# A quarter's tokens in three tiles of 128 lanes instead of four of 96, and a residual buffer that is loaded with bias and text

## The chip, the cores and the metric

The kernel runs on one NeuronCore of a Trainium2 chip. The metric is device time in microseconds for one execution; each kernel is run several times, and the median counts. The profiled execution is one more run, with the hardware profiler on. PE is TensorE (matmuls) and PEld its weight loads, DVE is VectorE, ACT is ScalarE, POOL is GpSimd, SP is SyncE, which here issues DMAs.

## The reference

Sixteen images of 3 x 128 x 128 and a text of 32 tokens for each go through one block of width 192. Cut to what matters:

```python
t = conv16x16(x) + conv_b                       # (16, 64, 192): 64 patches an image
h = attention(t, heads=12, head_dim=16)         # q, k, v, softmax, values
h = h @ wo.T + bo                               # (16, 64, 192)
h = concatenate([h, txt], axis=1)               # (16, 96, 192)
h = h + mamba(layernorm(h))                     # in-projection to 2 x 384, causal conv of 4 taps, silu,
                                                # selective scan with 16 states along the 96 tokens, gate, out-projection
h = h + ffn(layernorm(h))                       # below
# ffn: two "bitlinear" layers with ternary weights and activations rounded to 8 bits per token
x_q = round_to_8_bits(rmsnorm(h, g_in));  up, gate = split(x_q @ w_in_q.T)      # 2 x 512
y   = silu(gate) * up
out = round_to_8_bits(rmsnorm(y, g_out)) @ w_out_q.T
```

Each image has L = 96 tokens in h: 64 of the image (NP) and 32 of the text (NT). The layer norms, the rounding scales and the feed-forward work on one token at a time; only attention and the mamba mixer (convolution and scan) mix tokens, and only within an image.

## The kernel before

**Tiles.** The work after attention is cut into NQ = 4 quarters of QB = 4 images, so QT = 384 tokens. The mixer holds its data with channels on the lanes and the 384 tokens of a quarter along the columns, in CT = 3 tiles of 128 channels. The residual h, the layer norms and the feed-forward hold tokens on the lanes: one tile for each image, 96 lanes, four tiles a quarter. `h` is [96, 16, 192]: lanes 0 to 63 are written by `add_bo` (attention's projection plus the bias `bo_bc`), lanes 64 to 95 by one DMA of the text.

**The front.** SP issues all loads in one queue, in the order written. TensorE computes the patch embedding for two halves of the images, then one small matmul `wsum` (it sums the absolute feed-forward weights over lanes, and waits for VectorE's reduce of those weights, lines 1180 and 1181), then q, k and v. Attention runs over PAIRS = 8 pairs of images in a loop that is staggered over the engines: `scores(i)`, `values(i-2)`, `turn_prob(i-1)`, `project(i-3)`, `turn_out(i-2)` on TensorE, `softmax_in`, `softmax_out` and `add_bo` on VectorE, `block_keys` on GpSimd. `project(p)` multiplies the turned attention output of each of the two images (64 columns each) with wo. The first quarter's normalization and projections are woven in from i = 5, and the second quarter's normalization follows attention (its steps are negative).

**The steps.** The selective scan of one quarter takes 24 steps (3 channel tiles times 8 pairs of states), 96 in all. A step g is: `times_b` on GpSimd (line 455), `decay` on ScalarE (two exponentials, line 994), `scan` on VectorE (line 1291), `guards` on ScalarE (two tanh, line 1003) and `guard_states` on VectorE (1297, 1300), the product with C on GpSimd (461) or for three of eight steps on VectorE (1306), and `sum_y` on TensorE (808). All other work is placed beside the steps by hand: the tables MIXER and FFN give for each piece the step at which its engine does it, counted from the start (MIXER) or from the end (FFN) of its quarter's scan. So the feed-forward of quarter q runs beside the scan of quarter q+1, and that of the last quarter after all steps. SCALAR_WORK counts ScalarE's extra instructions of a step. If their sum is 4 or more, the guards of later steps are not computed ahead there:

```python
upto = min(STEPS, g + (1 if scalar_work(g) >= 4 else 3), guarded + 2)
while guarded < upto:
    guards(guarded)
    guarded += 1
beside(g)
```

A planner (`banks_of_jobs`) gives every TensorE job of these tables the PSUM bank that comes free first by the tables' due steps; a job waits for the last reader of the job before it in its bank. Three banks serve the jobs during the steps.

**The feed-forward of a quarter**, in order: `out_proj` (TensorE, two jobs) and `add_out` (VectorE, line 1317), `spread` (bn_stats and bn_aggr, 1323 and 1326), `root_in` (GpSimd, 467), `center` and `gain_in` (GpSimd, 477 and 483; for the last quarter `center_last` on VectorE, 1335), `max_in` (1377), `scale_in` (GpSimd, 490 to 495), `quant_in` (ScalarE, 1012), `turn_q1` (transposes, 769) and `q1_out` (1022), the gate and up matmuls (583, two each of 512 columns), `silu_gate` (1032), `times_up` (1384), `square` (1039), `gain_out` (GpSimd, 499; last quarter VectorE, 1357), `max_out` (1388), `mean_square` and `scale_out` (GpSimd, 506 to 524; last quarter partly VectorE, 1363 to 1367), `quant_out` (1045), `turn_q2` (787), `q2_out` (1052), `ffn_out` (583) and `finish` (1396), then `store` (SP, 374). Nearly all of these are one instruction for each tile of tokens, so four a quarter. The layer norm in front of the mixer is `spread_b` (1239, 1242), `root` (430 to 433), `normed` (933), `turn` (709), `turned` (940).

## Time and profile before

| | |
|---|---|
| Median of 3 runs | 544.12 us (543.4 to 544.31) |
| Profiled execution | 544.86 us, of it the span from first to last instruction 543.0 us |
| PE busy | 409.1 us (75%) |
| VectorE busy | 415.1 us (76%) |
| ScalarE busy | 349.2 us (64%) |
| GpSimd busy | 373.5 us (69%) |
| Mean granted TensorE clock | 0.874 |

A share of busy time is an average over the front, the steps and the tail. In all rows times are microseconds from the start of the span, durations microseconds or, where marked, nanoseconds. "idle before" is the time that the engine stood still just before the instruction, and the arrow names what ended it. A granted clock of 1.00 is TensorE at 2.4 GHz, 0.50 is 1.2 GHz.

### The profile page before, as it was taken

The page shows a single profiled execution, that of the slowest core. Times are in us where ns is not written, and L with a number is a line of the kernel's source. Part 1 is how long each engine was busy: PE and PEld are TensorE (multiplying, and loading weights), DVE is VectorE, ACT ScalarE, POOL GpSimd, SP SyncE. Part 2 cuts the span into 40 slices and gives each one's busy share as a digit, 9 for nine tenths or more (in the row PEclk, how much of TensorE's full clock was granted, in tenths as well). Part 3 has the DMA queues.
Part 4 walks back from the last instruction along what each step waited for, and adds up shares of the span by engine and source line. Part 5 has one row for each costly group of instructions (what it writes and reads, how often), then busy time and mean ns, then how long its engine had stood idle before and what let it go on. Part 6 is the DMA issues. An engine that isn't in the chain of part 4 may idle for free.

```text
span 543.0 us, 5369 instructions
## 1 busy us (share of the span) xinstructions
PE 409.1 (75%) x1588; PEld 233.1 (43%) x1588; DVE 415.1 (76%) x513; ACT 349.2 (64%) x627; POOL 373.5 (69%) x290
## 2 busy tenths in 40 slices
PE   5999996877975959996577799867656854857664
PEld 1336664544532425563243456534323632423533
DVE  3242556234899999899999989799899899798543
ACT  1135444228678669678489869968966866992362
POOL 2025630017869889799879999987799999977410
PEclk9999999686989779997988899787878989986966
DMA  8900000047000037200003440000244000000000
GB/s 312 233 1 1 2 0 2 0 160 308 1 4 1 1 116 264 85 4 0 2 0 143 164 159 4 11 12 0 116 174 174 2 22 1 1 1 0 7 16 22
DMA packets 10414, 34.30 MB, mean 63 GB/s; under 512 B 2208, under 2 KB 5104, under 8 KB 10160
## 3 DMA queue, kind: packets, MB, share of 16 engines
q1 hardware_dynamic: 9984, 33.17, 17.5%
q10 hardware_dynamic: 400, 0.79, 0.4%
q8 instruction: 13, 0.21, 0.2%
q14 instruction: 17, 0.14, 0.1%
HBM read 32.57 MB, written 1.38 MB: 63 GB/s over the span
## 4 chain that ended last, share of the span: by engine, by line
POOL 30%; DVE 12%; issue 11%; ACT 11%; PE 9%; ACTq 0%; DVEq 0%; POOLq 0%
POOL big L455 14%; POOL big L461 9%; DVE PS L1291 5%; PE PS L583 4%; ACT PS L994 3%; ACT big L1003 3%; PE PS L808 3%; POOL big L499 2%; DVE big L1300 1%; PE PS L732 1%; DVE big L1306 1%; ACT L994 1%; ACT big L1045 1%; DVE big L1384 1%; PE PS L787 1%
## 5 line engine op out<-in xcount | busy, mean ns | idle before, releaser
L808 PE MATMUL PS<-big,eighth 128*128 128x384 f32 x384 | 172.1, 587 | 69.3 <-POOL big L461 68.7
L1291 DVE TENSOR_TENSOR_SCAN PS<-PS,big 128x768 f32<-128x768 f32 x96 | 168.5, 1755 | 17.2 <-ACT PS L994 14.8
L455 POOL TENSOR_TENSOR big<-big,bc 128x768 f32<-128x768 f32 x96 | 173.4, 1820 | 0.0
L808 PEld LDWEIGHTS PS<-big,eighth 128*128 128x128 f32 x384 | 83.2, 227 | 140.7 <-POOL big L461 88.5
L461 POOL TENSOR_TENSOR big<-big,bc 128x768 f32<-128x768 f32 x60 | 109.2, 1821 | 39.7 <-DVE big L1300 39.5
L994 ACT ACTIVATE PS<-big,Aneg 128x384 f32<-128x384 f32 x192 | 103.7, 572 | 41.7 <-DVE big L1306 28.4
L1003 ACT ACTIVATE big<-big,guard,Ahalf 128x380 f32<-128x380 f32 x192 | 122.2, 690 | 0.0
L1300 DVE SCALAR_TENSOR_TENSOR big<-big,PS 128x768 f32<-128x768 f32 x60 | 57.0, 950 | 5.8 <-ACT big L1003 0.5
L420 POOL TENSOR_TENSOR big<-bc,cst_sb 96x1536 f32<-96x1536 f32 x8 | 22.0, 2752 | 43.3 <-ACT bc L903 32.2
L583 PE MATMUL PS<-big,w_in_sb 96*128 96x384 f32 x96 | 43.8, 597 | 5.0 <-DVE big L1252 4.4
L583 PE MATMUL PS<-big 128*64 128x34 f32 (+3 forms) x416 | 43.7, 282 | 0.0
L583 PEld LDWEIGHTS PS<-big 96*64 96x64 f32 (+2 forms) x416 | 30.5, 145 | 16.3 <-issue 14.6
L1297 DVE SCALAR_TENSOR_TENSOR PS<-big,PS 128x768 f32<-128x768 f32 x36 | 34.6, 961 | 3.8 <-DVE PS L1291 0.5
L430 POOL TENSOR_SCALAR rstd<-bmv 96x4 f32<-96x4 f32 x4 | 1.8, 460 | 48.8 <-DVE bmv L1242 48.7
L1306 DVE TENSOR_TENSOR big<-PS,bc 128x768 f32<-128x768 f32 x36 | 34.1, 948 | 0.4
L583 PEld LDWEIGHTS PS<-big,w_in_sb 96*128 96x128 f32 x96 | 21.7, 232 | 21.8 <-issue 13.1
L805 PE MATMUL PS<-big,diagD 128*128 128x384 f32 x24 | 13.6, 658 | 22.4 <-DVE big L1312 22.4
L583 PE MATMUL PS<-bc 128*96 128x512 f32 x48 | 22.4, 630 | 6.4 <-DMA bc<-in_cw_dram 6.4
L732 PE MATMUL PS<-big,diagW 128*128 128x384 f32 (+3 forms) x72 | 24.3, 480 | 0.0
L1045 ACT ACTIVATE big<-big,magic 96x512 f32<-96x512 f32 x14 | 10.5, 804 | 21.1 <-POOL big L523 15.3
L1209 DVE TENSOR_REDUCE big<-PS 128x12 f32<-128x768 f32 x8 | 7.6, 952 | 21.5 <-PE PS L583 21.5
L1104 ACT ACTIVATE big<-PS 128x768 f32<-128x768 f32 x8 | 6.5, 808 | 26.8 <-PE PS L648 26.8
(151 smaller groups left out, 538.8 us busy)
## 6 DMA issues: line engine op xcount, KB each, us to landing
bc<-bc_rows SPq DMA_DIRECT2D x32, 768.0 KB, 4.3
bc<-in_x_cols_dram SPq DMA_DIRECT2D x3, 512.0 KB, 6.5
bc<-in_x_cols_dram SPq DMA_DIRECT2D x1, 1536.0 KB, 8.7
out_dram<-h SPq DMA_DIRECT2D x4, 288.0 KB, 2.7
big<-in_f_in_dram SPq DMA_DIRECT2D x1, 768.0 KB, 10.8
bc<-in_cw_dram ACTq DMA_DIRECT2D x1, 576.0 KB, 5.6
w_in_sb<-in_w_in_dram SPq DMA_DIRECT2D x1, 576.0 KB, 14.4
big<-in_f_out_dram SPq DMA_DIRECT2D x1, 384.0 KB, 11.9
```

The lines of the kernel that those rows point to most:

```text
L420: P.tensor_tensor(kbd[:, p % 2], kT[:, hf, :, c:c + 128].unsqueeze(2).broadcast_to([F, 2, HPT, 128]), headmask.unsqueeze(1).unsqueeze(3).b ...
L455: P.tensor_tensor(pair(vR[:, g % VRING]), part(du, q, m).unsqueeze(1).broadcast_to([128, PAIR, QT]), rows_of(g, 0), ALU.mult).then_inc(sem ...
L461: P.tensor_tensor(v, v, rows_of(g, 1), ALU.mult).then_inc(sem("c_pool"), 1)
L583: return pe.matmul(o_, l_, r_, start=start, stop=stop)
L732: ins = pe.matmul(o_[:, :, s:L], diagW[:, j, KW - 1 - s, :], xi[:, :, 0:L - s], start=False, stop=s == KW - 1, skip_group_check=True)
L808: ins = pe.matmul(y_sum, eighth[:, :], vR[:, g % VRING, QT * e:QT * (e + 1)], start=False, stop=True, skip_group_check=True)
L994: ins = A.activation(state_of(g, e), part(delta, q, m), ACT.Exp, scale=Aneg[:, PAIR * j + e, m:m + 1])
L1003: ins = A.activation(gR[:, g % GRING, QT * e:QT * (e + 1)].rearrange("p (b l) -> p b l", b=QB)[:, :, 0:L - 1], lt[:, :, 1:L], ACT.Tanh, bi ...
L1291: V.tensor_tensor_scan(h_, h_, vR[:, g % VRING], 0.0, ALU.mult, ALU.add).then_inc(sem("scan_done"), 1)
L1297: V.scalar_tensor_tensor(states(g), gR[:, g % GRING], 1.0, states(g), ALU.add, ALU.mult).then_inc(sem("guarded_here"), 1)
L1300: V.scalar_tensor_tensor(vR[:, g % VRING], gR[:, g % GRING], 1.0, states(g), ALU.add, ALU.mult).then_inc(sem("guarded"), 1)
L1306: V.tensor_tensor(pair(vR[:, g % VRING]), pair(states(g)), rows_of(g, 1), ALU.mult).then_inc(sem("c_vector"), 1)
```

## The change

The 384 tokens of a quarter are laid out without a gap: token t of the quarter is lane t mod 128 of tile t div 128, so there are NTL = 3 tiles of 128 lanes, and an image may lie in two of them. Everything that holds tokens on the lanes follows: h is [128, 12, 192], and xn, xq, sg, yf, the statistics and the scales have three tiles. The transposes are 128 wide, and the jobs of out_proj, q1, q2 and the down projection hold two tiles in the first and one in the second. In the tables the gates are all at step 14 (the fourth was at 15), and SCALAR_WORK has 3 for 4 where a piece lost an instruction (5 for 6 for silu).

The bias is no longer added from a buffer. h is loaded with bias rows (five DMAs) and text rows (four DMAs), all in front of the loads of the feed-forward weights. `project` multiplies whole tiles of 128 tokens: aoT holds the four images of a quarter with 96 columns each, the text's columns set to zero once by GpSimd, so that the product is zero there. Even pairs do tile 0, odd pairs tiles 1 and 2, and `add_bo` adds the product to what h holds.

```diff
+NTL = QT // 128
-for b in range(QB):
-    FFN.update({"gate%d" % b: 14 + b // 3, "up%d" % b: 16 + b // 2, "times%d" % b: 17 + b // 2, "square%d" % b: 18 + b // 2,
-                "gain%d" % b: 19 + b // 2, "max%d" % b: 21 + b // 2})
+for i in range(NTL):
+    FFN.update({"gate%d" % i: 14, "up%d" % i: 16 + i // 2, "times%d" % i: 17 + i // 2, "square%d" % i: 18 + i // 2,
+                "gain%d" % i: 19 + i // 2, "max%d" % i: 21 + i // 2})
-SCALAR_WORK = dict(xn=4, turned=2, ..., quant_in=4, q1_out=2, silu=6, square0=1, square1=1,
-                   square2=1, square3=1, quant_out0=2, quant_out1=2, q2_out0=2, q2_out1=2)
+SCALAR_WORK = dict(xn=3, turned=2, ..., quant_in=3, q1_out=2, silu=5, square0=1, square1=1, square2=1, quant_out0=2,
+                   quant_out1=1, q2_out0=2, q2_out1=1)
...
-        g_in_bc = sb("g_in_bc", [F, D])
-        g_out_bc = sb("g_out_bc", [F, FH])
-        bo_bc = sb("bo_bc", [NP, D])
+        g_in_bc = sb("g_in_bc", [128, D])
+        g_out_bc = sb("g_out_bc", [128, FH])
...
-        h = sb("h", [L, NB, D])
+        h = sb("h", [128, NQ * NTL, D])
...
-        aoT = carve(256, F).rearrange("p (m t) -> p m t", m=2)
+        aoT = carve(2 * QT, F).rearrange("p (m b l) -> p m b l", m=2, b=QB)
...
+        def tiles(q, i=slice(0, NTL)):
+            return h[:, NTL * q:NTL * (q + 1)][:, i]
...
             load("wo", wo_sb, wo)
-            load("wo", bo_bc[:, :], bo.partition_broadcast(NP))
+            parts = h[:, :, :].rearrange("p (q i) d -> p q i d", i=NTL)
+            text = txt.rearrange("(q b) l d -> b l q d", b=QB)
+            for i, rows, n in ((0, 0, 64), (0, 96, 32), (1, 0, 32), (1, 64, 64), (2, 32, 64)):
+                load("txt", parts[rows:rows + n, :, i, :], bo.unsqueeze(0).unsqueeze(0).broadcast_to([n, NQ, D]))
+            for b, i, rows in ((0, 0, 64), (1, 1, 32), (2, 2, 0), (3, 2, 96)):
+                load("txt", parts[rows:rows + NT, :, i, :], text[b])
             load("ffn", f_in_raw, f_in.rearrange("p m n -> p (m n)"))
             load("ffn", f_out_raw, f_out.rearrange("p m n -> p (m n)"))
-            load("txt", h[NP:L, :, :], txt.rearrange("b l d -> l b d"))
...
             link(P.memset(vbd, 0.0))
+            link(P.memset(aoT, 0.0))
...
             def project(p):
-                for b2 in range(2):
+                turned_all = aoT.rearrange("p m b l -> p m (b l)")
+                for k, i in enumerate((1, 2) if p % 2 else (0,)):
                     for m in range(2):
-                        ins = mm(project_out[:, D * b2:D * b2 + D], aoT[:, m, 64 * b2:64 * b2 + 64], wo_sb[:, m, :],
+                        ins = mm(project_out[:, D * k:D * (k + 1)], turned_all[:, m, 128 * i:128 * (i + 1)], wo_sb[:, m, :],
                                  m == 0, m == 1)
...
             def out_proj(q, j):
-                for b2 in range(2):
-                    t = L * (2 * j + b2)
+                for k, i in enumerate((2,) if j else (0, 1)):
                     for m in range(CT):
-                        ins = mm(o_[0:L, D * b2:D * b2 + D], part(sres, q, m)[:, t:t + L], w_out_sb[:, m, :],
+                        ins = mm(o_[:, D * k:D * (k + 1)], part(sres, q, m)[:, 128 * i:128 * (i + 1)], w_out_sb[:, m, :],
                                  m == 0, m == CT - 1)
...
             def normed(q):
-                for b in range(QB):
-                    ins = A.activation(xn[:, b, :], h[:, QB * q + b, :], ACT.Identity, bias=nmr[:, b:b + 1],
-                                       scale=rstd[:, b:b + 1])
+                for i in range(NTL):
+                    ins = A.activation(xn[:, i, :], tiles(q, i), ACT.Identity, bias=nmr[:, i:i + 1], scale=rstd[:, i:i + 1])
...
             def add_bo(p):
                 dve.wait_ge(sem("wo_ps"), p + 1)
-                V.tensor_tensor(h[0:NP, 2 * p:2 * p + 2, :], project_out.rearrange("p (b c) -> p b c", b=2),
-                                bo_bc[:, :].unsqueeze(1).broadcast_to([NP, 2, D]), ALU.add).then_inc(sem("h_sb"), 1)
+                if p == 0:
+                    dve.wait_ge(sem("ld_txt"), 16 * LOADS["txt"])
+                here = tiles(p // 2, slice(1, 3) if p % 2 else slice(0, 1))
+                n = 2 if p % 2 else 1
+                V.tensor_tensor(here, project_out[:, 0:D * n].rearrange("p (i c) -> p i c", i=n), here, ALU.add
+                                ).then_inc(sem("h_sb"), 1)
```

All other functions of the feed-forward and of the normalization change in the same way as out_proj and normed: loops over three tiles of 128 lanes for loops over four of 96, in the same order and with the same waits.

## Rows read from the trace of the kernel before

**Rows 1.** Busy time of each engine in one stretch of steps; then clock, DMA share, GB/s.

```profile
232.00:329.00 97.00, 75.41 (x228) 42.63 (x227) 92.73 (x98) 75.49 (x139) 88.15 (x73) 0.89 0.18 66
```

The columns are: stretch, its length, busy us (and instructions) of PE, PEld, DVE, ACT and POOL, granted clock, DMA share, GB/s.

**Rows 2.** Groups of instructions by line, steps only (129 to 504 us).

```profile
L461 POOL TENSOR_TENSOR big<-big,bc 128x768 f32<-128x768 f32 x60 | 109.2, 1821 | 39.7 <-DVE big L1300 39.5
```

**Rows 3.** The chain that ended last, in the steps: start, us, what.

```profile
246.01 1.47 POOL big L477
...
253.60 1.76 POOL big L483
...
285.09 1.14 DVE bst L1239 x4
...
458.12 1.86 ACT big L1012 x4
...
460.96 2.42 ACT big L1003 x4
...
468.79 2.41 ACT big L1032 x4
...
491.36 2.45 POOL big L499 x2
```

**Rows 4.** DMA queues and DMA issues with size and us to landing.

```profile
q1 hardware_dynamic: 9984, 33.17, 17.5%
...
h<-in_txt_dram SPq DMA_DIRECT2D x1, 384.0 KB, 13.4
```

**Rows 5.** The timeline of the loads: start, us, engine, line, what.

```profile
9.29 0.47 SPq L346 DMA_DIRECT2D h<-in_txt_dram  x1
...
20.65 2.28 DVE L1180 TENSOR_REDUCE wsum<-big 96x1 f32<-96x2048 f32 x1 [6.93 <-DMA big<-in_f_out_dram]
...
22.85 0.94 DVE L1181 TENSOR_REDUCE wsum<-big 128x1 f32<-128x768 f32 x1
...
28.72 0.28 PE L583 MATMUL PS<-wsum,ones 128*128 128x2 f32 x2
```

**Rows 6.** The timeline of TensorE and ScalarE in attention, and one output projection.

```profile
66.06 1.51 PE L583 MATMUL PS<-big 96*64 96x192 f32 x8
...
94.90 2.78 PE L583 MATMUL PS<-big,w_in_sb 96*128 96x384 f32 x4 [3.36 <-DVE big L1252]
...
102.64 1.48 PE L648 MATMUL PS<-cst_sb,big 128*128 128x128 f32 x6
...
122.73 1.86 ACT L933 ACTIVATE big<-h,nmr,rstd 96x192 f32<-96x192 f32 x4 [3.11 <-POOL nmr L433]
...
332.61 2.11 PE L583 MATMUL PS<-w_out_sb,big 128*96 128x192 f32 x12
```

**Rows 7.** Busy time and granted clock in three short stretches, columns as in rows 1.

```profile
94.90:106.00 11.10, 11.10 (x46) 7.13 (x46) 0.91 (x3) 1.86 (x2) 0.00 (x0) 0.54 0.00 0
...
302.50:324.90 22.40, 22.37 (x65) 13.09 (x66) 20.25 (x21) 14.89 (x30) 21.99 (x18) 0.92 0.49 177
...
517.30:525.80 8.50, 8.22 (x24) 4.27 (x24) 2.03 (x4) 6.39 (x11) 0.00 (x0) 0.54 0.01 2
```

**Rows 8.** The timeline of the tail.

```profile
507.05 2.93 ACT L1045 ACTIVATE big<-big,magic 96x512 f32<-96x512 f32 x4 [13.83 <-POOL big L523]
...
512.53 1.39 DVE L1335 SCALAR_TENSOR_TENSOR big<-h,big,g_in_bc 96x192 f32<-96x192 f32 x4
...
518.90 6.70 PE L583 MATMUL PS<-f_in_q,big 96*96 96x512 bf16 x16
...
528.76 2.45 DVE L1388 TENSOR_REDUCE big<-big 96x1 f32<-96x512 f32 x4
...
530.05 0.20 POOL L510 TENSOR_TENSOR big<-big 96x4 f32<-96x4 f32 x1
...
532.91 2.88 PE L787 MATMUL PS<-cst_sb,big 96*128 96x96 f32 x16 [7.31 <-ACT big L1045]
...
535.59 2.76 PE L583 MATMUL PS<-f_out_q,big 128*96 128x192 bf16 x16
```

More of the change, by code:

```diff
@@ L551, in beside @@
                         scale_in(q)
-                for b in range(QB):
+                for b in range(NTL):
                     for q in due("gain%d" % b, g):
@@ L707, in turn @@
                     o_ = begin("turn", q, m)
-                    for b in range(QB):
-                        ins = pe.transpose(o_[0:F, L * b:L * b + L], xn[:, b, F * m:F * (m + 1)], ident[0:L, 0:L])
+                    for i in range(NTL):
+                        ins = pe.transpose(o_[0:F, 128 * i:128 * (i + 1)], xn[:, i, F * m:F * (m + 1)], ident)
                     done(ins, "turn")
@@ L834, in beside @@
                 for kind in ("gate", "up"):
-                    for b in range(QB):
+                    for b in range(NTL):
                         for q in due("%s%d" % (kind, b), g):
@@ L1010, in quant_in @@
                 act.wait_ge(sem("q1_scale"), q + 1)
-                for b in range(2 if q == LAST else QB):
-                    ins = A.activation(xq[:, b, :], xq[:, b, :], ACT.Identity, bias=magic[0:L, 0:1],
+                for b in range(2 if q == LAST else NTL):
+                    ins = A.activation(xq[:, b, :], xq[:, b, :], ACT.Identity, bias=magic[:, 0:1],
                                        scale=st[:, q, 6, b:b + 1])
-                    if b % 2:
+                    if b:
                         ins.then_inc(sem("q1_ready"), 1)
@@ L1078, in beside @@
                 for q in due("silu", g):
-                    for b in range(QB):
+                    for b in range(NTL):
                         silu_gate(q, b)
-                for b in range(QB):
+                for b in range(NTL):
                     for q in due("square%d" % b, g):
@@ L1087, in beside @@
                             quant_out(q, 2 * half)
-                            quant_out(q, 2 * half + 1)
+                            if half == 0:
+                                quant_out(q, 1)
                 for half in range(2):
@@ L1091, in beside @@
                         q2_out(q, 2 * half)
-                        q2_out(q, 2 * half + 1)
+                        if half == 0:
+                            q2_out(q, 1)
             for i in range(PAIRS + 3):
@@ L1237, in spread_b @@
                     dve.wait_ge(sem("xn_ready"), q)
-                for b in range(QB):
-                    ins = V.bn_stats(bst[:, b, :], h[:, QB * q + b, :])
+                for b in range(NTL):
+                    ins = V.bn_stats(bst[:, b, :], tiles(q, b))
                 link(ins)
-                for b in range(QB):
+                for b in range(NTL):
                     ins = V.bn_aggr(bmv[:, b, :], bst[:, b, :])
@@ L1314, in add_out @@
             def add_out(q, j):
[L1315 removed]
                 job_here(dve, "out", q, j)
[L1317 to L1318 removed]
+                here = tiles(q, slice(2, 3) if j else slice(0, 2))
+                n = 1 if j else 2
+                V.tensor_tensor(here, job_bank("out", q, j)[:, 0:D * n].rearrange("p (i c) -> p i c", i=n), here, ALU.add
+                                ).then_inc(sem("left_out"), 1)
             def spread(q):
                 job_left(dve, "out", q, 1)
[L1322 to L1323 removed]
+                for b in range(NTL):
+                    ins = V.bn_stats(dst[:, b, :], tiles(q, b))
                 link(ins)
[L1325 removed]
+                for b in range(NTL):
                     ins = V.bn_aggr(dmv[:, q, b, :], dst[:, b, :])
@@ L1435, in after @@
                         quant_in_last(q)
-                for b in range(QB):
+                for b in range(NTL):
                     for q in due("times%d" % b, g):
                         times_up(q, b)
-                for b in range(QB):
+                for b in range(NTL):
                     for q in due("gain%d" % b, g):
@@ L1442, in after @@
                             gain_last(q, b)
-                for b in range(QB):
+                for b in range(NTL):
                     for q in due("max%d" % b, g):
```

164 lines of the change are left out of this document (77 added, 87 removed), and 6 rows, old and new, of the table PE_JOBS.

## The prediction, written before the kernel was changed

> **What bounds the kernel now.** I read the windows by stage first, then the groups of instructions inside the step stage, then the chain that ended last, and the timeline only where the chain runs through work that the change touches. The kernel has three stages. The front (patch embedding, attention, the first quarter's projections) lasts until the first scan at 129 us. The steps (96 of them, 24 a quarter) last until 504.3, and the tail (feed-forward of the last quarters) until 543.0.
>
> In the steps VectorE is nearly full: 92.7 of 97.0 us in the stretch of the second quarter, with GpSimd at 88.2 and ScalarE at 75.5 [rows 1]. In the 375 us of steps GpSimd's product with C waits 40 us for VectorE [rows 2]. So VectorE sets the pace most of the time, GpSimd is close behind, and each small feed-forward instruction between two steps delays a scan or a product. The chain shows the same: it changes engine, and it passes through feed-forward work wherever that stands in front of a step's own work [rows 3]. In the tail there are no steps left to hide anything. The chain runs through single instructions in turn, with TensorE near half its clock, 0.54 and so mostly at the lower of its two levels [rows 7, 8].
>
> **The front: loads.** Before, one load of the bias (48 KB) and, behind the feed-forward weights, one of the text (384 KB, 512 packets of 768 bytes). After, nine loads ahead of those weights: 1,024 packets of bias and 512 of text. The weights are what DVE sums at 20.65, when the last of them lands; the sum ends at 23.79 and TensorE needs it at 28.72 for its small matmul, ahead of all of q and k [rows 5]. That is 4.9 us; TensorE loads the weights of that matmul 0.4 earlier, so the slack is 4.5 us. The text was issued at 9.29 [rows 5] and landed after 13.4 [rows 4], at 22.7. It lies directly behind the weights that landed at 20.65, so its 512 packets took 2.1 us, 4.1 ns each. By that the weights land later by 512 + (1,024 − 64) = 1,472 packets, 6.0 us: **TensorE waits 1.5 us**. Lower bound: under 3.1 ns a packet there is no wait at all, 0. Upper bound: the mean packet of the queue in the whole execution, over 3 KB, took 0.175 × 543 × 16 / 9,984 = 152 ns of one engine of 16, or 9.5 ns [rows 4]. A packet of 768 bytes should not cost more: 14.0 us, a wait of 9.5 us. I take the row of the text, which is the same kind of packet. The seven more issues on SP (about 0.5 us each, as the text's 0.47 [rows 5]) are passed while the queue has older data to move. What stands behind the wait: all q and k, then all of attention, so the wait counts in full.
> The text load priced a packet at 4.1 ns [rows 4, 5]. The Trainium skill (DMA: Bandwidth & Descriptors, section "Why small descriptors are slow") gives a fixed overhead of about 3 cycles beside 32 bytes a cycle, which makes 27 cycles of 850 MHz for 768 bytes, an estimate of 2.0 ns over 16 engines. By that the weights would be 2.9 us late, inside the slack, and the forecast 1.5 us lower.
>
> **The front: attention.** In its steady part TensorE runs without a gap, and a projection of a pair is four matmuls (eight records) in 1.51 us, the records 0.18 apart [rows 6]. After, even pairs have two matmuls and odd ones four. They load 128 columns of weights where they loaded 64. The mixer's output projection, with 96 columns of weights and the same 192 moving, had twelve records in 2.11, again 0.18 each [rows 6], so I price the wide ones at 0.18 too. Four even pairs save 0.72 each: −2.9. The project of pair 6 lies ahead of pair 7's transpose in TensorE's order, so it counts too. Bound: if wider loads showed, +0.05 a record, it would be −0.5 less for the even pairs and 1.6 more for the odd ones, −0.8 in all. Behind attention lies the normalization of the second quarter, which the first scan waits for: four bn_stats become three (−0.28) with one bn_aggr less (−0.1), by the group of four in 1.14 [rows 3], and xn 4 to 3 of 1.86 [rows 6], −0.5. The six wide transposes cost what eight narrow ones did (low clock: 1.48 for six of 128 columns [rows 6]). Normalization −0.9, and together with the loads the front gives −2.9 − 0.9 + 1.5 = **−2.3**. Hidden at nothing: the memset of aoT, one instruction of 768 columns on GpSimd, which then idles until the keys are there (uncovered it would be under 2 us, by g_out's 512 columns in 1.22 [rows 3]), and the wider g loads.
>
> **The steps.** I take the pieces on the chain [rows 3] one by one. I price an instruction of GpSimd, VectorE or ScalarE by its columns, not by its lanes, so a group of four becomes three, and a width of 768 becomes 576. Bound: if 128 lanes cost more than 96 in proportion, nothing is saved here (rival B). For columns speaks GpSimd's product on 96 lanes and 768 columns, 1.76, beside the product with C on 128 lanes and 768, 109.2 / 60 = 1.82 [rows 2, 3].
> - center 1.47 and gain_in 1.76, once each in the shown quarter and again in the third (440.3, 445.3): −0.36 and −0.44, twice: −1.6
> - bn_stats four in 1.14: −0.28
> - quant_in, four in 1.86: −0.46
> - silu, four in 2.41: −0.60
> - second pair of gain_out, two in 2.45 at 491.4: −1.22
> - The weights in SCALAR_WORK: quant_in goes from 4 to 3 and so under the threshold of 4. ScalarE then does a guard ahead of quant_in, in a wait for GpSimd's scales, and not two behind it. At 460.96 four guard activations in 2.42 become two: −1.2.
>
> Sum **−5.4**. Bounds: off the chain too the work shrinks, by about 7.7 us on VectorE (12 to 9 each of the products with up and the maxima, the statistics, add_out, max_in, finish) and 6.1 on GpSimd, so no more than −7.7. At the other end the neighbours just off the chain hold the pace, and one guard now precedes xn at step 18: 0 to +0.8. I take the chain's own sum: it is the sum of what stood in front of a step. The gates of a quarter all come at step 14 and the bank planner has one job less to seat, so I see no new wait for a bank.
>
> **The tail**, from the scales at 507.05 [rows 8]. quant_out 4 to 3 of 2.93: −0.73; two q2_out of 512 columns for 384: +0.2. center 4 to 3 of 1.39, one finish less, the maximum over 576: −0.33 − 0.33 − 0.2. First q1 transposes (four, now 128 wide, 0.25 for 0.19 at low clock) and their eviction: +0.34. So TensorE begins the gates 1.05 earlier. Its 16 records of 512 columns in 6.70, 0.427 each, become 12: −1.71. Then three gains and maxima for four on VectorE, −1.23, but GpSimd's mean square ends at 530.25 where VectorE's maxima end at 531.22. Only 0.97 counts, then GpSimd ends last. q2 transposes 16 in 2.88, now 12 of 128 columns at 0.247: +0.08. Down projection 16 records of 0.16 to 12: −0.64. Last finish one for two: −0.33. Sum: **−4.6**. Bounds: −5.5 if GpSimd's first small operations, slow beside VectorE's gains, speed up; −3 if the wider transposes and evictions show twice.
>
> **Sum.** −2.3 − 5.4 − 4.6 = −12.3 us against a span of 543.0 with 1.9 us around it (544.86). The median shown is 544.12, 0.74 lower; I put the same difference on it: **531.8 us**, 2.3% faster. What a measurement tells from no change is 0.2%, 1.1 us.
>
> **The rivals.**
> - *A, the loads hurt.* The bias packets cost up to the mean packet, and TensorE waits 4 to 9.5 us: 534 to 539.8. For it: the loads are in front, the queue is full until 26 us, all 1,024 packets read the same 768 bytes. Against it: the text's rate. 0.13.
> - *B, the steps give nothing.* The engines are coupled, and what one saves it waits for the other, as it does for 40 us already [rows 2]: 531.8 + 5.4 = 537.2. For it: VectorE and GpSimd are only 5 us apart in 97 [rows 1]. Against it: both lose work. 0.15.
> - *C, more than the chain shows.* VectorE's whole 7.7, no wait in front: 528; and if attention keeps TensorE's clock up at 94.9 to 106, where it ran 11.1 us at 0.54 [rows 7], up to 4 less: 525. 0.12.
> - *D, slower: TensorE's clock.* Place: the steps with the convolutions of the next quarter. From 302.5 to 324.9 TensorE was busy 22.37 of 22.40 at 0.92 [rows 7], so it is the bound there. In the front TensorE was idle for 3.4 us before 94.9 [rows 6], and at 0.54 for the next 11 us though never idle [rows 7]. The change takes TensorE work out just before these steps. If one such stretch ran at half clock, it would take 22.4 × 0.92 / 0.5 = 41.2, +18.8: 550.6. From 12.3 us of it the kernel is slower. Against it: the four-matmul groups right after the idle there recover in one step. 0.08. The Trainium skill (TensorE: Matmul & The Clock Gate, section "HAM oscillation") states that gaps between bursts of matmuls throw the clock back to half; the front's rows agree.
>
> The forecast itself has 0.52, with its own range 529 to 535 (the load 0 to 3, the steps −7.7 to −3). The range that is to hold 8 in 10 reaches over A, B and C: 525 to 540. Faster: the forecast, A, B, C, less 0.01 for A and B together, 0.91; same 0.02; slower, most of D, 0.07.
>
> **What would show it.** In the trace after: the reduce of f_in begins near 26.7 (not 20.65) and the matmul with wsum near 30.3. The projections of even pairs have four records. First scan near 127. Per quarter nine matmuls of out_proj, three gates, three ups. The last scan's quarter ends near 497, gates in the tail 12 records, tail from the last gate to the end 34 us for 38.7. Wrong would be: a wait above 4 us at wsum; GpSimd's or VectorE's idle time in the steps up by 5 us; a granted clock below 0.8 in the steps' windows.

## The result

The changed kernel took 541.70 us (median of 20 runs, 536.07 to 545.06), the kernel before 545.08 beside it (20 runs, 543.03 to 550.84). The ratio is 0.9901, 95% interval 0.9876 to 0.9926: 1.0% faster, where 2.3% were forecast, and the median lies 1.7 us above the range. (Ratios, and below the median of e15_all_back, leave out the few executions that ran disturbed, so a ratio is not the quotient of the two medians.) The profiled execution took 541.64 with a span of 539.8; before it was 544.86 and 543.0.

**The loads.** First the timeline of the changed kernel: start, us, engine, line, what.

```profile
7.28 3.29 SPq L350 DMA_DIRECT2D h<-in_bo_dram  x5
10.61 5.89 SPq L350 DMA_DIRECT2D h<-in_txt_dram  x4
16.54 3.72 SPq L350 DMA_DIRECT2D big<-in_f_in_dram  x1
20.31 3.71 SPq L350 DMA_DIRECT2D big<-in_f_out_dram  x1
...
37.31 2.28 DVE L1192 TENSOR_REDUCE wsum<-big 96x1 f32<-96x2048 f32 x1 [23.62 <-DMA big<-in_f_out_dram]
39.51 0.94 DVE L1193 TENSOR_REDUCE wsum<-big 128x1 f32<-128x768 f32 x1
...
40.50 0.59 PE L593 MATMUL PS<-wsum,ones 128*128 128x2 f32 x2 [10.70 <-DVE wsum L1193]
```

The feed-forward weights land at 37.31 where they landed at 20.65 [rows 5], and TensorE stands still for 10.70 us. Then the windows of the same kernel: stretch, length, VectorE busy (and instructions), granted clock, DMA share, GB/s.

```profile
12.00:14.00 2.00, 1.69 (x9) 1.00 1.04 304
14.00:16.00 2.00, 0.00 (x0) 1.00 0.52 135
16.00:18.00 2.00, 0.00 (x0) 1.00 0.20 46
18.00:20.00 2.00, 0.00 (x0) 1.00 0.17 60
20.00:22.00 2.00, 0.00 (x0) 1.00 0.16 50
22.00:24.00 2.00, 0.00 (x0) 1.00 0.26 53
24.00:26.00 2.00, 0.00 (x0) 1.00 0.31 72
26.00:28.00 2.00, 0.00 (x0) 1.00 0.57 176
28.00:30.00 2.00, 0.00 (x0) 1.00 1.09 180
30.00:32.00 2.00, 0.00 (x0) 1.00 1.05 208
32.00:44.00 12.00, 6.48 (x12) 0.50 0.72 158
44.00:60.00 16.00, 3.17 (x5) 0.95 0.00 1
```

From 16 to 26 us, while the bias comes in, the queue moves about 56 GB/s with its engines busy for 0.22 of the time. Behind TensorE's idle time the granted clock is 0.50 until past 44, so the first projections run at the lower of its two levels.

**The tail** of the changed kernel, by the timeline, beside [rows 8]:

```profile
507.20 0.56 DVE L1326 TENSOR_TENSOR big<-PS,big 128x384 f32<-128x384 f32 x1 [3.53 <-PE PS L817]
...
509.66 2.23 ACT L1053 ACTIVATE big<-big,magic 128x512 f32<-128x512 f32 x3 [12.97 <-POOL big L533]
...
520.48 5.30 PE L593 MATMUL PS<-f_in_q,big 96*128 96x512 bf16 x12 [0.41 <-ACT big L1030]
...
531.81 2.82 PE L797 MATMUL PS<-cst_sb,big 128*128 128x128 f32 x12 [6.02 <-ACT big L1053]
...
534.56 2.10 PE L593 MATMUL PS<-f_out_q,big 128*128 128x192 bf16 x12
...
536.06 1.07 DVE L1410 SCALAR_TENSOR_TENSOR h<-PS,big,h 128x192 f32<-128x192 f32 x3 [4.62 <-PE PS L593]
```

Compare starts and sizes. The gates, 16 records in 6.70 us, are 12 in 5.30. They began 1.58 later than before; the down projection 1.03 earlier.

Three points cut the execution into stages: TensorE's matmul with wsum, the first scan, and VectorE's last gate by z (L1326, before L1312).

| stage | before | after | change | forecast |
|---|---|---|---|---|
| start to wsum matmul | 28.72 | 40.50 | +11.8 | +1.5 |
| wsum matmul to first scan | 100.40 | 99.29 | −1.1 | −3.8 |
| first scan to last gate by z (the steps) | 375.20 | 367.41 | −7.8 | −5.4 |
| last gate by z to end (the tail) | 38.68 | 32.60 | −6.1 | −4.6 |
| span | 543.0 | 539.8 | −3.2 | −12.3 |

The steps and the tail gave more than forecast. The loads took most of it back, and the lower clock behind them hides what attention gave in the second row; both are taken apart below. Each column is one profiled execution. In GpSimd's row of [rows 2] little moved:

```profile
L471 POOL TENSOR_TENSOR big<-big,bc 128x768 f32<-128x768 f32 x60 | 109.5, 1824 | 37.3 <-DVE big L1314 37.1
```

It waits 37.3 us for VectorE, not 39.7: the steps are shorter, and in this row the same engine is waited for.

### The profile page after: what moved, and what is told of

The parts are those of the page before. It is cut to its first block, busy times and chain, and to the rows that moved or that the text cites. A ratio compares the mean times of both kernels' runs of the same rounds, so it can differ in the third digit from the quotient of the medians.

```text
span 539.8 us, 5082 instructions
## 1 busy us (share of the span) xinstructions
PE 397.8 (74%) x1484; PEld 222.7 (41%) x1484; DVE 399.8 (74%) x481; ACT 338.3 (63%) x601; POOL 367.3 (68%) x288
## 4 chain that ended last, share of the span: by engine, by line
POOL 31%; DVE 11%; PE 9%; issue 9%; ACT 6%; DVEq 0%; ACTq 0%; POOLq 0%
POOL big L465 15%; POOL big L471 10%; DVE PS L1305 5%; PE PS L817 4%; PE PS L593 3%; POOL big L509 2%; ACT PS L1001 2%; DVE big L1314 1%; PE PS L743 1%; DVE big L1320 1%; POOL big L447 1%; DVE big L1399 1%; ACT big L1053 1%; ACT big L1010 1%; PE PS L797 1%
## 5 line engine op out<-in xcount | busy, mean ns | idle before, releaser
L817 PEld LDWEIGHTS PS<-big,eighth 128*128 128x128 f32 x384 | 81.9, 224 | 144.8 <-POOL big L471 93.6
L471 POOL TENSOR_TENSOR big<-big,bc 128x768 f32<-128x768 f32 x60 | 109.5, 1824 | 37.3 <-DVE big L1314 37.1
L593 PEld LDWEIGHTS PS<-big 128*64 128x64 f32 (+3 forms) x400 | 31.6, 155 | 15.6 <-issue 15.3
L440 POOL TENSOR_SCALAR rstd<-bmv 128x3 f32<-128x3 f32 x4 | 1.9, 464 | 46.5 <-DVE bmv L1256 46.4
L1053 ACT ACTIVATE big<-big,magic 128x512 f32<-128x512 f32 x11 | 8.4, 805 | 18.8 <-POOL big L533 14.2
## 6 DMA issues: line engine op xcount, KB each, us to landing
h<-in_bo_dram SPq DMA_DIRECT2D x3, 192.0 KB, 15.1
```

The costliest lines, as they stand in the source:

```text
L471: P.tensor_tensor(v, v, rows_of(g, 1), ALU.mult).then_inc(sem("c_pool"), 1)
L593: return pe.matmul(o_, l_, r_, start=start, stop=stop)
L817: ins = pe.matmul(y_sum, eighth[:, :], vR[:, g % VRING, QT * e:QT * (e + 1)], start=False, stop=True, skip_group_check=True)
```

## Experiments on the front: which packets, and why

Four kernels, each the changed one with only the nine loads altered.

*e1_last*: the nine loads behind all others.

```
-            parts = ...; for i, rows, n in ...: load("txt", ...)   (nine loads)
             load("ffn", f_in_raw, ...)
...
             load("g", g_out_bc[:, :], g_out.partition_broadcast(128))
+            parts = ...; for i, rows, n in ...: load("txt", ...)   (the same nine)
```

> The changed kernel with its nine bias and text loads moved behind all other loads; nothing else. Theory (the nine loads in front of the FFN weights cost the whole front loss, and the rest of the change is worth what the first scan to the end showed, 13.9 us): FFN weights land near 20.6, the wsum matmul is near 28.7, the q/k projections run at the clock of the kernel before, the first scan is at 125 to 127, and the span is 527 to 530 (about 529 to 532 as a time), 2.3 to 2.9% under the kernel before. Rival (the front loss comes from the attention or from the clock on its own): the first scan stays near 139.8 and the time near 541. Rival (a late start gave the steps their gain, so it is lost with the stall): first scan near 126, but steps and tail give back only 10, span near 533.

*e2_distinct*: the same destinations, other sources.

```
-    load("txt", parts[rows:rows + n, :, i, :], bo.unsqueeze(0).unsqueeze(0).broadcast_to([n, NQ, D]))
+    load("txt", parts[rows:rows + n, :, i, :], txt.rearrange("b l d -> (b l) d")[0:NQ * n].rearrange("(q n) d -> n q d", q=NQ))
```

> The changed kernel, its five bias loads in place with the same destinations and the same 1,024 packets of 768 bytes, but each packet reads a row of its own (rows of the text tensor) instead of the one bias row: the true bias is left out. Theory (many packets that read the same 768 bytes are slow): the FFN weights land at 21 to 27, the first scan is 8 to 13 us earlier than in the changed kernel (127 to 132), time 529 to 534. Rival (packet count, or the small lane ranges of the nine loads): no change, FFN weights near 37, time near 541.

*e3_one*: one bias load in place of five, `load("txt", h[:, 0:8, :], bo...broadcast_to([128, 8, D]))`, text into `h[32 * b:32 * (b + 1), 8:12, :]`.

> The changed kernel with the five bias loads joined into one over all 128 lanes and two thirds of h (the same 1,024 packets of the same row) and the four text loads put into the last third of h (the same 512 packets); bias and text lie at wrong places. Theory (same address): FFN weights land at 33 to 38 as in the changed kernel. Rival (number of loads, or narrow lane ranges): they land at 21 to 27 and the first scan comes 8 us or more earlier.

*e4_bias_last*: only the five bias loads behind the others.

> The changed kernel with the five bias loads behind all other loads, the four text loads still in front. Theory (same address): the text loads cost only their packets, 512 at 4 to 9.5 ns, 2 to 5 us: FFN weights at 21 to 26, first scan 125 to 129, time 528 to 533. Rival (lane ranges of 32, packet count): FFN weights at 25 to 30, a third to half of the loss stays.

What was measured; of the front, the start of the sum over f_in (weights landed), the wsum matmul and the first scan; e1_last timed in 6 runs (the profiled one, 525.86, is the fastest of them), the others once, which is why the landing of the weights and not the time decides here:

| kernel | weights | wsum matmul | first scan | span | time |
|---|---|---|---|---|---|
| before | 20.65 | 28.72 | 129.12 | 543.0 | 544.86 |
| changed | 37.31 | 40.50 | 139.79 | 539.8 | 541.64 |
| e1_last | 20.36 | 28.60 | 124.60 | 524.1 | 526.85 (525.86 to 531.50) |
| e2_distinct | 26.94 | 30.19 | 126.85 | 527.1 | 528.88 |
| e3_one | 36.92 | 40.11 | 141.07 | 541.5 | 543.35 |
| e4_bias_last | 21.37 | 29.42 | 126.06 | 525.7 | 527.55 |

The ratio of e1_last to the kernel before is 0.9661 (0.9614 to 0.9708), and its span is 3 us under the 527 to 530 expected. What lay behind the stall was not lost with it: from the first scan to the end it took 399.50, the changed kernel 400.01. The two readings that decide are these. The timeline and a window of e2_distinct, columns as above:

```profile
26.94 2.28 DVE L1192 TENSOR_REDUCE wsum<-big 96x1 f32<-96x2048 f32 x1 [12.85 <-DMA big<-in_f_out_dram]
```

```profile
14.00:26.00 12.00, 0.09 (x1) 1.00 1.09 237
```

And the windows of e3_one; its columns are stretch, length, busy us (and instructions) of PE, PEld, DVE, ACT and POOL, clock, DMA share, GB/s:

```profile
16.00:18.00 2.00, 2.00 (x6) 0.78 (x5) 0.00 (x0) 0.00 (x0) 0.00 (x0) 1.00 0.30 59
18.00:20.00 2.00, 2.00 (x6) 0.69 (x5) 0.00 (x0) 0.68 (x1) 0.00 (x0) 1.00 0.53 52
```

With 1,024 different source rows the queue is full and moves 237 GB/s. With the one row it moves 46 to 72, whether the packets go out in five narrow loads or in one over all 128 lanes. So neither the number of loads, nor their lane ranges, nor the count of packets is the cause, but their source: all 1,024 read the same 768 bytes of bo. Against e2_distinct the weights are 10.4 us later, 10.1 ns for each bias packet. In e4_bias_last, with only the text in front, the weights landed at 21.37; in the ten traces with no such load in front, at 20.1 to 20.8. The 512 text packets by themselves cost about 1 us, 2 ns each. Then two more.

*e6_rows4*: the bias loads' source becomes `txt[0, 0:NQ, :].unsqueeze(0).broadcast_to([n, NQ, D])`.

> The changed kernel, its bias loads in place with the same destinations and 1,024 packets of 768 bytes, but the four quarters of h read four different neighbouring rows (one block of 3,072 bytes, each row 256 times) instead of one row 1,024 times; the true bias is left out. With one row the loads ran at 50 to 60 GB/s and the weights landed at 37.3, with 1,024 different rows at 26.9. Theory (the reads queue at the one place in memory that holds the row, so four rows serve four times as fast): full rate or nearly, weights at 26.9 to 29, time 528 to 532. Rival (any source read again and again is slow): weights at 35 to 37, time 540 to 542.

*e9_before_loads*: the kernel before and one load.

```
+            load("txt", h[0:NP, :, :], bo.unsqueeze(0).unsqueeze(0).broadcast_to([NP, NB, D]))
             load("ffn", f_in_raw, ...)
```

> The kernel before plus one load in front of the feed-forward weights: the bias row into 64 lanes and 16 rows of h, 1,024 packets of 768 bytes that all read one row; it is overwritten later, so the result is the same. Theory (these packets alone are the front's loss, at 12 to 14 ns each): weights land 11 to 14 us later (32 to 35), less 4.5 of slack, so first scan 7 to 13 us later with the low clock behind the stall, span 550 to 556. Rival (the loss needs the change's other parts): under 2 us.

In e6_rows4 the weights landed at 25.82: four neighbouring rows, each read 256 times, are as quick as 1,024 different ones. It is enough that the reads are spread over 3,072 bytes instead of 768; why, no run here shows. One rival is left: e2_distinct and e6_rows4 read the text tensor, and no run reads one row of it 1,024 times, so the place where bo lies is not told apart from the repetition. The front of e6_rows4 was good (first scan 125.57), and yet it took 532.15 us; the steps were longer, and a section below says by what. In e9_before_loads one load of the same row made the kernel before 12.9 us longer (span 555.9, time 557.77): weights at 36.12, wsum matmul at 39.32, first scan at 141.96. So the load alone does it, 15.5 us for 1,024 packets or 15.1 ns each, and nothing else of the change is needed. That is more than was expected for the weights (32 to 35) and the upper end for first scan and span. How busy the engines show says little here. One of its windows, columns as in the first table of windows:

```profile
18.00:20.00 2.00, 0.00 (x0) 1.00 0.62 53
```

That is 53 GB/s at a share of 0.62, where the changed kernel moved 60 at 0.17.

**The clock behind the stall.** From the wsum matmul to the first scan e1_last, e2_distinct and e4_bias_last took 96.00, 96.66 and 96.64 us; the changed kernel and e3_one, where TensorE had stood idle for 10.7 and 10.9 us, took 99.29 and 100.96. In the kernel before it took 100.40, and 102.64 in e9_before_loads. So behind the stall it took 2.2 to 4.4 us more, 2.7 in the changed kernel, and there the granted clock stood at 0.50 before it came back to 1.00 by 46. The Trainium skill (TensorE: Matmul & The Clock Gate, section "HAM oscillation") states that idle gaps throw the clock to half; the trace agrees, 1.00 before the gap and 0.50 behind it.

## Experiments on the steps: whose work was it

*e7_nudge* tests a single place. Twelve times VectorE sums delta over the later positions with a scan on 384 columns (L1283, the suffix scan here; 0.92 us at its shortest). Before, one of them took 5.23 us, by the timeline:

```profile
256.25 5.23 DVE L1283 TENSOR_TENSOR_SCAN big<-keep,big 128x384 f32<-128x384 f32 x1
```

In the changed kernel the same one took 1.36, and the suffix scan behind it came 4.1 us earlier, counted from the first scan, where this one came 0.5 earlier. Edit, on e1_last, in gain_in:

```
+                if q == 0:
+                    P.tensor_tensor(spare[:, :], g_out_bc[:, 0:D], g_in_bc[:, :], ALU.mult)
                 P.tensor_tensor(xq, xq, g_in_bc[:, :].unsqueeze(1)..., ALU.mult)
```

> The changed kernel with its nine loads last, plus one GpSimd product of 192 columns (0.4 to 0.6 us, into a spare tile) just ahead of the gain of quarter 0, so that this stretch of GpSimd is about as long again as with 768 columns; the result is the same. Theory (3.6 us of the gain in the steps come from one place: before, VectorE's suffix scan at 256.25 was held for 5.2 us behind three GpSimd products in a row, and the shorter gain lets it in between them): the suffix scan near 251.6 takes about 5 us again, the scans after it are 3.5 to 4.5 us later, span 527.5 to 528.5 for 524.1. Rival (the gain comes from the work taken out and not from the meeting): the suffix scan stays at 1.3 us and the span grows by 0 to 0.6.

The nudge did not bring the hold back: the suffix scan took 1.89 us, and from the first scan to the end e7_nudge took 399.81 for 399.50. So it doesn't tell what a hold there costs. e9_before_loads does, as it is the kernel before in its steps. That scan took 1.75 in it (its longest were 4.24 and 2.84 elsewhere), and its steps took 375.99 for 375.20. Such a hold comes and goes with small shifts, and this one place isn't what the change saved. Holds as a whole may have a part in it, which no run isolates: the twelve suffix scans together took 21.2 us in the kernel before and 20.9 in e9_before_loads, and 17.6 to 19.6 in the kernels with the change, but for the two in which one took over 8 us.

That it is a hold is best seen in e6_rows4, by the timeline of VectorE and GpSimd:

```profile
169.46 2.64 POOL L447 TENSOR_TENSOR big<-big 128x1152 f32<-128x1152 f32 x1
170.07 8.13 DVE L1297 TENSOR_TENSOR_SCAN big<-keep,big 128x384 f32<-128x384 f32 x1
172.04 1.82 POOL L471 TENSOR_TENSOR big<-big,bc 128x768 f32<-128x768 f32 x1
173.81 3.58 POOL L465 TENSOR_TENSOR big<-big,bc 128x768 f32<-128x768 f32 x2
```

A scan that takes 0.92 alone started behind a GpSimd product and ended at 178.20, 0.8 after the fourth of four that followed each other without a gap. From the first scan to the last gate by z this kernel took 370.54, the others of its kind 366.8 to 367.8, 3 us too much. Its tail took 34.19 for 32.6, but that is no hold: its last output projection took 5.76 us for 3.17, at the lower clock (more on this below). The Trainium skill (SBUF — State Buffer, section "Who interferes with whom") states that a VectorE instruction with two SBUF inputs contends with a GpSimd instruction that reads SBUF, and calls what they share an exclusive lock. The trace agrees: keep and delta both lie in SBUF. That GpSimd then keeps the turn through four instructions no page says, and no run here isolates it.

*e8_guard* tests the prediction's −1.2 for the order of the guards. Edit, on e1_last: `xn=3` to `xn=4` and `quant_in=3` to `quant_in=4` in SCALAR_WORK.

> The changed kernel with its nine loads last and the weights of xn and quant_in in the list of ScalarE's work at 4 each, as in the kernel before, so that beside these two one guard more stands behind them and none ahead. Prediction's step: this order gives 1.2 us back in the quarter shown, so the span grows by 1.2, up to 3 times that where the other quarters behave alike: 525.3 to 527.5. Rival (VectorE and GpSimd, not ScalarE, hold the pace at these steps): no difference over 0.3, 524 to 524.4.

Its median was 528.47 (526.56 to 528.90), ratio 0.9658 (0.9625 to 0.9690) as e1_last's 0.9661. From first scan to last gate it took 367.65. Its profiled span, 526.9, lies in the range expected if the order counted, but so does that of the same kernel without the edit: e1_last once more (e13_last_again) had 526.7. The three traces of e1_last's kernel took 366.82, 367.53 and 367.31 for the steps, so beside them the order of the guards costs 0.1 to 0.8 us, which can't be told from nothing.

Then the work was given back, one engine at a time, on e1_last, for the three quarters whose feed-forward lies in the steps:

```
e10 (GpSimd)   + P.tensor_tensor(spare[:, 0:80], ...)  ahead of center and of gain_in
               + if b == 2: P.tensor_tensor(spare[:, :], yf[:, b], g_out_bc[:, :], ALU.mult)
e11 (VectorE)  + a fourth bn_stats, bn_aggr, product with up and maximum; 192 columns of add_out, finish
e12 (ScalarE)  + a fourth xn, quant_in, silu, square, quant_out
e14 (TensorE)  - for k, i in enumerate((2,) if j else (0, 1)):
               + for k, i in enumerate(((2, 2) if q < LAST else (2,)) if j else (0, 1)):
               (in out_proj and ffn_out; ffn_in of tile 2 twice too)
e15            all four together (GpSimd's third product 352 columns wide for 512)
```

> The changed kernel with its nine loads last, and in the quarters whose feed-forward work lies in the steps GpSimd gets back about the work that three tiles for four took from it: products of 80 columns (0.37 us) ahead of center and gain_in, one of 512 columns (1.22 us) ahead of the third gain_out, all into a spare tile, 3 x 1.96 = 5.9 us. By the prediction's pieces on the chain GpSimd's part of the steps' gain was 1.6 + 1.2 = 2.8 us: time 529.6 for 526.8. Theory now (GpSimd paces the steps as much as VectorE): 4 to 6 us, 531 to 533. Rival (it is slack): under 1 us.

> As the run before, but the work given back is VectorE's: in three quarters a fourth bn_stats and bn_aggr, a fourth product with up (0.7), a fourth maximum (0.6), 192 columns more of add_out and of finish, into a spare tile, 2.4 us a quarter, 7.1 in all. By the prediction VectorE's part on the chain was 0.3 us: time 527.1. Theory now (VectorE is nearly full, so its work counts nearly in full, and the 7.2 to 7.8 us of the steps' gain are mainly this): 4 to 7 us, 531 to 534. Rival (slack): under 1 us.

> As the two before, but the work given back is ScalarE's: a fourth xn, quant_in, silu, square and quant_out in the quarters whose work lies in the steps, 0.46 + 0.46 + 0.6 + 0.6 + 0.7 = 2.8 us a quarter, 8.5 in all. By the prediction quant_in and silu are on the chain, 1.06 us in the quarter shown, up to 3.2 for three: time 527.9 to 530. Rival (ScalarE, 73 of 95 us busy, is slack): under 1 us, 526.5 to 527.8.

> The changed kernel with its nine loads last, once more and unchanged, as the one that the three before are compared with on the same chip. Expected: 526 to 528.5 us as before; in its trace the twelve suffix scans of VectorE (0.92 us where GpSimd is idle) take other times than in its first trace, if what holds them is the chance of how they meet GpSimd's products, and the scans after them shift by the difference; if the durations are a fixed part of the program they are the same within 0.1 us.

> The changed kernel with its nine loads last, and in the three quarters whose feed-forward work lies in the steps TensorE makes the matmuls of the third tile twice (three more of out_proj, two more of gate, of up each, four more of the down projection), which is about the work that three tiles for four took from it: some 0.5 + 1.7 + 0.3 = 2.5 us a quarter at the lower clock, 1.5 at the higher. Theory (TensorE is the bound in the steps with the convolutions and behind the gates): 1.5 to 4 us longer than its partner. Rival (VectorE and GpSimd hold the pace): under 1 us.

> The extra work of the four runs together (GpSimd's third product 352 columns wide, the spare tiles of bfloat16). If the shares add up: 4.6 us for three engines plus TensorE's 0 to 3, 533 to 536 for 528. If engines that wait for each other hide each other's work when one alone is loaded, the sum is larger than its parts: 6 to 9 us, near the 7.2 to 7.8 that the steps gained, 534.5 to 537. Rival (the gain came from something that is not work, such as how VectorE's suffix scans meet GpSimd's products): under 4 us.

> The changed kernel with its nine loads last, unchanged, as the partner of the two others on the same chip: 526.5 to 528.6 us. Its suffix scans take again slightly different times, and the last scan comes 375.2 minus 7 to 8 us after the first.

| kernel | median of its runs | ratio to before | to its partner |
|---|---|---|---|
| e13_last_again (partner of the next three) | 528.61 (524.06 to 528.85) | 0.9648 (0.9597 to 0.9699) | |
| e10_pool_back | 528.19 (527.75 to 532.42) | 0.9680 (0.9632 to 0.9728) | −0.4 |
| e11_dve_back | 532.00 (531.25 to 532.36) | 0.9733 (0.9690 to 0.9776) | +3.4 |
| e12_act_back | 529.85 (529.00 to 534.13) | 0.9713 (0.9660 to 0.9765) | +1.2 |
| e16_last_third (partner of the next two) | 527.96 (525.68 to 528.63) | 0.9658 (0.9620 to 0.9695) | |
| e14_pe_back | 530.13 (527.98 to 531.27) | 0.9701 (0.9663 to 0.9739) | +2.2 |
| e15_all_back | 533.59 (531.91 to 535.43) | 0.9774 (0.9734 to 0.9814) | +5.6 |

The last column is a difference of medians of six runs that scatter by 1 to 5 us, so a difference under about 2 us is no more than a hint. The intervals overlap too, but for e15_all_back against its partner. What can be said: the four shares sum to 6.4, the four together cost 5.6, so they add up roughly. No sign is there of one engine hiding another's work, though the scatter would allow it; and 5.6 compares with the 7.8 that the steps gained. VectorE's share is the largest, and all six of its executions are longer than all six of its partner's. GpSimd's, which the prediction put at 2.8 and the new theory at 4 to 6, shows in no median, but stays open: in its profiled execution the steps took 371.57, 4.0 more than the partner's, and that execution, 532.42, was 3 to 5 us longer than the five others.

In the profiled executions part of VectorE's and ScalarE's cost is TensorE's clock. The timeline and a window of TensorE in e12_act_back, at its last output projection:

```profile
493.39 5.17 PE L594 MATMUL PS<-w_out_sb,big 128*128 128x192 f32 x18 [0.74 <-DVE big L1337]
```

```profile
493.00:498.00 5.00, 4.61 (x16) 0.55 0.00 0
```

The same in its partner e13_last_again:

```profile
494.83 3.17 PE L593 MATMUL PS<-w_out_sb,big 128*128 128x192 f32 x18 [0.74 <-DVE big L1326]
```

```profile
494.50:499.00 4.50, 4.17 (x27) 1.00 0.00 0
```

Eighteen records in 5.17 us at a granted clock of 0.55, in 3.17 at 1.00. Ahead of the matmuls before it TensorE had been idle 2.53 us instead of 1.37. The same projection took 5.97 in e11_dve_back, behind 3.05 of idle time, and 5.76 in e6_rows4, behind 2.53. But the length of that wait alone does not decide: behind 2.04 in e14_pe_back and 3.38 in e10_pool_back it took 3.17 and 3.16. Tails: 34.52 for ScalarE's run and 34.74 for VectorE's, 32.57 for the partner, so 2 us of each lie in the tail. In the steps VectorE's work cost 370.14 − 367.53 = 2.6 us and ScalarE's 0.2. Whether the 5.6 of e15_all_back hold such 2 us too, no trace of it tells.

## Why the prediction was wrong

**The step that failed is the price of a bias packet.** It said: "I take the row of the text, which is the same kind of packet", 4.1 ns, and "A packet of 768 bytes should not cost more" than 9.5. A load of 1,024 such packets by itself took 15.1 ns each (e9_before_loads), and TensorE stood still for 10.70 us where a wait of 1.5 was forecast. The weights came 16.7 us later for 1,472 packets, 11.3 ns each on the mean. Split by e2_distinct: where each packet reads a row of its own the weights land at 26.94, forecast 26.7, wsum matmul at 30.19, forecast 30.3, first scan at 126.85, forecast 127. For such packets the price came out, 4.3 ns on the mean, but with luck. The text packets cost about 2 ns each (e4_bias_last) and so the 1,024 others 5.4. And TensorE did not wait at all in e2_distinct: it reached the wsum matmul only at 30.19 because its patch embedding took 23.60 us for the 22.44 before. In three traces of e1_last's kernel it took 22.35, 23.55 and 23.35, so that 1 us is a difference between executions. The bias packets are another kind: same size, same lanes, but one source row, which adds 10.1 ns each. The text said that "all 1,024 packets read the same 768 bytes" and put it in rival A, with 0.13, but let the bound go by the mean packet of the queue. That bound was none: it held only for packets that read different memory, and the wait passed rival A's 4 to 9.5 us too. And the trace before had a load to price it by. Its bo_bc was that same row, 64 times. The issues by the timeline, then by the DMA view with KB and us to landing:

```profile
7.01 0.45 SPq L346 DMA_DIRECT2D big<-in_wo_dram  x1
7.50 0.56 SPq L346 DMA_DIRECT2D bo_bc<-in_bo_dram  x1
```

```profile
big<-in_wo_dram SPq DMA_DIRECT2D x1, 144.0 KB, 8.2
bo_bc<-in_bo_dram SPq DMA_DIRECT2D x1, 48.0 KB, 8.6
```

So wo landed at 15.2 and bo_bc at 16.1. An estimate from these rows is 0.9 us for 64 packets, 14 ns each. It is a rough one, as loads overlap, but it stands above the bound of 9.5 and close to what was measured.

**What stands behind the wait.** That all of q and k, and so the whole front, moves by the wait was right: of the 11.8 at wsum 10.70 are the idle time, and 0.9 the longer patch embedding of this execution (23.34 us). Not in the sum: the lower clock behind such a stall, 2.7 us. Loads term in all: +11.8 + 2.7 = +14.5 for +1.5, with 96.6 as the undisturbed length of the stretch.

**Attention and normalization**, −3.8: right in sum. Undisturbed, that stretch took 96.0 to 96.7 us for 100.40, so −3.7 to −4.4. The timeline of the changed kernel shows an even and an odd pair:

```profile
75.20 0.82 PE L593 MATMUL PS<-big 96*128 96x192 f32 x4
...
79.66 1.47 PE L593 MATMUL PS<-big 96*128 96x192 f32 x8
```

Wide records at 0.18, as priced; the bound of +0.05 each was not needed. (It was added up wrongly too: 16 records of even pairs and 32 of odd ones make 2.4, so the bound is −0.5 and not −0.8.)

**The steps**, −5.4 with a bound of −7.7: sized too small, measured −7.8 (−7.5 to −8.4 in e1_last, its two repeats, e2_distinct, e4_bias_last, e7_nudge and e8_guard), against one trace of the kernel before; against e9_before_loads, its steps once more, it is 0.8 more. The sum by pieces on the chain was wrong inside. The guards' order gave at most 0.8, which can't be told from nothing, for 1.2. GpSimd's 2.8 shows in no median. VectorE, priced at 0.3 with the rest left to the bound, carried 2.6 in the steps (3.4 by the medians); TensorE, not priced at all, about 2 (a hint). How the 7.8 split over the engines stays open beyond that. A chain names one engine at a time, and where two are 5 us apart in 97 [rows 1] the neighbour's work can count as well. Rival B (the steps give nothing) did not happen, nor D: in the steps the granted clock was 0.86 on the mean, for 0.87 before.

**The tail**, −4.6: measured −6.1. From quant_out to the gates −1.03 (forecast −1.05), from the gates to the q2 transposes −2.68 (−1.71 − 0.97 = −2.68), from the down projection to the end of the last finish −0.98 (−0.97), the first two from the starts in [rows 8] and above. The exact −2.68 is luck: up to the first gain it gave 1.50 and not 1.71 (from 518.90 to 526.35, now from 520.48 to 526.43), and the gains and maxima 1.20 and not 0.97, since VectorE's maxima still ended last (530.09, GpSimd's mean square 529.85). The store was not in the sum: from the last finish to the end it took 3.86 us and now 2.67. The 128 rows of a tile now follow each other in memory, and a store's median landing went from 2.7 to 2.3 us; that was not tried by itself. But the last store of the kernel before took 3.4 us to land, and 2.7 in e9_before_loads, whose tail was 37.9 for 38.7. So 0.7 of the 1.2 belong to that one execution, and the tail gained nearer 5.3 than 6.1.

**The time.** 539.8 − 530.7 (543.0 − 12.3) = 9.1 us too long: loads +13.0, steps −2.4, tail −1.5. With no wait for the loads the forecast would have been 530.3; e1_last took 526.85, 528.61 and 527.96 in its three sets of runs.

**A better version** follows: the changed kernel with its nine loads last. Three times six runs gave 0.9661, 0.9648 and 0.9658 of the kernel before, 3.4 to 3.5% faster. Nobody needs bias and text before attention's projections are added, near 60 us; the queue of e1_last is quiet from 36 on (2 GB/s), so in this place they cost nothing. The row of one source stays slow there too, 72 GB/s in e1_last between 26 and 32 us, but nobody waits.

## What to carry to other kernels

Price a transfer by its source as well as by size and count: before a small row is broadcast by many packets, look for a load in the trace that really reads one place again and again, however small (here bo_bc, 64 packets), and where there is none, leave the upper end open. Put a load behind whatever somebody waits for soonest, by when its own reader comes; moving nine loads made 541.7 us into 527 to 529. When pieces on a chain are summed, allow for the near neighbour's work, and distrust a piece that is only a change of order. When a forecast number comes out, look whether its parts did.

## What the hardware showed that was not expected

- 1,024 packets of 768 bytes that read one row moved at about 50 to 60 GB/s (15.1 ns each in e9_before_loads, beside 4.3 on the mean in e2_distinct, where bias and text packets read different rows); four neighbouring rows were enough for full speed.
- A VectorE scan with both inputs in SBUF took 0.92 us at its shortest and up to 8.13 while four GpSimd products ran in a row; how they meet differs between executions of one kernel (the suffix scan near 45 us behind the first scan took 2.84 in e1_last and 2.06 in e13_last_again), which may be a part of the scatter of 524 to 531 us.
- TensorE's granted clock fell to 0.50 behind 10.7 us of idleness. In the tail one output projection took 3.16 or 3.17 us in some executions and 5.17 to 5.97 in three, with nearly the same work in front; what decides is not isolated.
- The patch embedding took 22.35, 23.55 and 23.35 us in three traces of one kernel, so its first scan moved from 124.60 to 126.60; single traces are not compared closer than that.
